# Cross attention, the first head pair's maxima: half the score units copied by ScalarE, and a running maximum by a scan over a PSUM unit and a copied unit

## The chip, the cores and the metric

One core of one Trainium2 chip runs the whole program: six stages of a small perceiver-like network on 128 tokens of width 256 with a context of 12,544 tokens. The metric is the device time of one execution in microseconds (us), as the median of several runs.

## The reference, cut to what matters

The change lies in the fourth stage, the cross attention of the 128 tokens over the 12,544 context tokens, with 16 heads of 16 numbers each. It is an exact softmax attention over the whole context:

```python
def _L1_xattn_ref(q, k, v, Wq, bq, Wo, bo):
    H, E = 16, 16                       # 128 rows of q, 12544 rows of k and v
    qp, kp, vp = ((a @ Wq.T + bq) for a in (q, k, v))      # split into heads
    scores = jnp.einsum('blhe,bshe->bhls', qp, kp)
    attn = jax.nn.softmax(scores / np.sqrt(E), axis=-1)
    out = jnp.einsum('bhls,bshd->blhd', attn, vp)
    return out @ Wo.T + bo

x = x + _L1_xattn_ref(_layernorm(x), ctx_1024, ctx_1024, L1_xattn_Wq, L1_xattn_bq, L1_xattn_Wo, L1_xattn_bo)
```

## The kernel before

The kernel is one program with one instruction list for each engine, and the lists are tied together by counting semaphores: an instruction adds one to a semaphore when it ends, and another engine's list waits until the count is reached. Each engine works through its list in the order in which it is written.

The heads are treated in eight pairs (NG = 8). For each pair s the kernel needs, for each of the 128 query rows and both heads, the largest score over all 12,544 keys, before it can take exponentials. So each pair passes twice over the keys, once for the maxima and once for the exponentials and the weighted sum.

The maxima pass cuts the keys into 28 units (UNITS) of 448 columns (MU). `maximum_group` (L854 on, matmul in L866) lets TensorE multiply a unit: two matmuls, one for each head, that use different rows of the array, into two neighbouring PSUM banks. The ring `max_ring` gives even units banks 0 and 1 and odd units banks 2 and 3 (MAX_SLOTS = (0, 2)). On VectorE `reduce_unit` (L1610 on) waits for the unit (c_max), reduces 2 x 448 scores to two negated maxima in `unit_max` (L1616), and adds one to c_red, for which TensorE waits before it uses the same banks again. After the 28th unit one small reduction (L1622) takes the minimum of the 28 negated maxima to `neg_max` and counts c_hm.

On TensorE `turn_maxima` (L876) waits for c_hm and transposes `neg_max` to one row; ScalarE's `maxima_row` (L1173) copies that row into `q_stack`, so that the second pass's matmuls subtract the maxima by themselves. The second pass is `scores` (L889, TensorE), `exponentials` (L1180, ScalarE) and `weigh` (L905, TensorE).

The order of the whole is written out. TensorE first does the 28 units of pair 0, then the first 4 units of pair 1 (LEAD = 2 groups of two units), then `turn_maxima(0)`. From then on `step_plan` mixes, step by step, three exponential tiles of pair s, their weighing and a few maxima units of pair s + 1. So the maxima of pairs 1 to 7 are taken beside the exponentials of the pair before; those of pair 0 have no such work beside them. ScalarE's first instruction in the stage is `maxima_row(0)`. Before the stage VectorE splits the queries and writes `q_max` (L1602) and `q_stack` (L1604). `prob` is a large SBUF tile of 12 buffers (NPB) that `exponentials` fills; it is unused during pair 0's maxima. SyncE loads the keys (`k_stack`) and values (`vals`) of pairs 0 and 1 ahead; `load_keys` for later pairs waits for scores of the pair whose buffer it takes.

Of the kernel before, what the change touches and what calls it, by code (L numbers as in the profile page):

```python
# [23 lines left out]
ALU = mybir.AluOpType  # L24
ACT = mybir.ActivationFunctionType
AX_X = mybir.AxisListType.X

P = 128
# [8 lines left out]
MIN_START = -3.0e38  # L37
# [19 lines left out]
NG = H // 2  # L57
VW = HD + 1
TILES = S // P
MU = 448  # L60
UNITS = S // MU
# [14 lines left out]
MAX_SLOTS, EXP_BANKS, SUM_BANK = (0, 2), (4, 5, 6), 7  # L76
# [22 lines left out]
def wait_at(eng, sem, value):  # L99

    if isinstance(value, int) and value <= 0:
        return
    eng.wait_ge(sem, value)
# [139 lines left out]
def build_kernel(nc, k_scratch, v_scratch, ones_scratch, ctx_t, x_in, mask_in, const_in, hist_in, l0_in, rows0_in, xw_in, x_bo_in, x_o_in, l1_in, rows1_in, v_in,  # L243
                 tables_in, out):
    with ExitStack() as outer:  # L245
        def sem(name):
            return outer.enter_context(nc.semaphore(name))

        def sb(name, shape, dt=F32, scope=outer):
            return scope.enter_context(nc.sbuf_tensor(name, shape, dt))  # L250


        bank = outer.enter_context(nc.psum_tensor("bank", [P, 8, 512], F32))
# [121 lines left out]
        le = ExitStack()  # L375
# [3 lines left out]
        q_max = sb("q_max", [P, NG, T], F32R, scope=le)  # L379
        q_stack = sb("q_stack", [P, NG, 2 * T], F32R, scope=le)  # L380
        unit_max = sb("unit_max", [P, 2, UNITS, 2], scope=le)
        neg_max = sb("neg_max", [P, 2, 32], F32R, scope=le)
        o_part = sb("o_part", [P, NG, T], scope=le)
        acc = sb("acc", [P, NG, 2, VW], scope=le)
# [3 lines left out]
        prob = sb("prob", [P, NPB, 2, 2 * T], scope=le)  # L388
# [81 lines left out]
        c_max, c_red, c_hm, c_nt = sem("c_max"), sem("c_red"), sem("c_hm"), sem("c_nt")  # L470
        c_sc, c_exp, c_wt = sem("c_sc"), sem("c_exp"), sem("c_wt")
        c_ev, c_ot, c_fill, ld_rows0 = sem("c_ev"), sem("c_ot"), [sem("c_fill0"), sem("c_fill1")], sem("ld_rows0")
        c_ones = sem("c_ones")

        exp_ring = Ring(EXP_BANKS)
        exp_at, turn_at = {}, {}
# [120 lines left out]
        def _(pe):  # L597
# [254 lines left out]
            max_ring = Ring(MAX_SLOTS)  # L852

            def maximum_group(g):  # L854

                s = g // (UNITS // 2)
                for u in (2 * g % UNITS, 2 * g % UNITS + 1):
                    n, at = max_ring.take()
                    wait_at(pe, c_red, max_ring.free(n))
                    if u == 0 and s < 2:  # L860
                        pe.wait_ge(c_fill[s], 32)
                    if u % CHUNK_UNITS == 0:
                        pe.wait_ge(c_stack[s % 2][u // CHUNK_UNITS], 96 * (s // 2 + 1))
                    cols = slice(u * MU, (u + 1) * MU)
                    for hh, rows in ((0, slice(0, 3 * HD + 1)), (1, slice(64, 64 + 3 * HD))):
                        last = nc.tensor.matmul(bank[:, at + hh, 0:MU], q_max[rows, s, :], k_stack[s % 2][rows, cols],  # L866
                                                start=True, stop=True)
                    last.then_inc(c_max, 1)
# [25 lines left out]
            def weigh(e):  # L894

                s, u = divmod(e, EU)
                pe.wait_ge(c_exp, exp_at[e][0] + 1)
                if u == 0:
                    pe.wait_ge(c_vals[s % 2], 16 * (s // 2 + 1))
                    wait_at(pe, c_ev, s)  # L900
                for t in range(2):
                    k = 2 * u + t
                    for hh in range(2):
                        at = 32 * (2 * hh + t)
                        last = nc.tensor.matmul(bank[at:at + 32, SUM_BANK, 0:T],  # L905
                                                vals[:, s % 2, hh, k * VW:k * VW + 32],
                                                prob[:, e % NPB, t, hh * T:(hh + 1) * T],
                                                start=(u == 0), stop=(u == EU - 1))
                last.then_inc(c_wt, 1)

            dve_s.wait(pe, "q_max")
            for g in range(UNITS // 2):
                maximum_group(g)
            for g in range(UNITS // 2, UNITS // 2 + LEAD):
                maximum_group(g)
            turn_maxima(0)
            waiting = []
            for exps, turns, groups in step_plan():
                for e in exps:
                    scores(e)  # L920
                done_now = []
                for e in waiting:
                    if done_now and e % EU == 0:
                        break
                    weigh(e)
                    done_now.append(e)
                waiting = waiting[len(done_now):] + list(exps)
                for s in turns:
                    turn_maxima(s)
                for g in groups:  # L930
                    maximum_group(g)
            for e in waiting:
                weigh(e)
            pe.wait_ge(c_red, NG * UNITS)
            for g in range(NG):
                pe.wait_ge(c_ev, g + 1)
                last = nc.tensor.transpose(bank[:, g // 4, (g % 4) * P:(g % 4 + 1) * P], o_part[:, g, :], ident)
# [74 lines left out]
        def _(act):  # L1012
# [8 lines left out]
            A = nc.scalar.activation  # L1021
# [145 lines left out]
            def maxima_row(s):  # L1167

                n, at = turn_at[s]
                act.wait_ge(c_sc, n + 1)  # L1170
                if s == 0:
                    dve_s.wait(act, "q_stack")
                A(q_stack[MAX_ROW:MAX_ROW + 1, s, :], bank[MAX_ROW:MAX_ROW + 1, at, 0:2 * T],  # L1173
                  ACT.Copy).then_inc(c_exp, 1)
# [8 lines left out]
            def sums_copy(s):  # L1183
                act.wait_ge(c_wt, EU * (s + 1))
                A(o_part[:, s, :], bank[:, SUM_BANK, 0:T], ACT.Copy).then_inc(c_ev, 1)

            maxima_row(0)
            ready = None
            for exps, turns, groups in step_plan():
# [95 lines left out]
        def _(dve):  # L1285
            V = nc.vector
            own = [0]

            def link(ins):

                own[0] += 1
                ins.then_inc(dve_own, 1)
                dve.wait_ge(dve_own, own[0])
# [146 lines left out]
            for b in range(4):  # L1440
# [4 lines left out]
                                            op0=ALU.mult, op1=ALU.mult), f"att0_{b}")  # L1445
# [51 lines left out]
            for b in range(4):  # L1497
# [37 lines left out]
                                        op1=ALU.add), "x2")  # L1535
# [11 lines left out]
                                        op0=ALU.is_equal, op1=ALU.add))  # L1547
# [59 lines left out]

            max_ring = Ring(MAX_SLOTS)

            def reduce_unit(s, u):  # L1610

                n, at = max_ring.take()
                dve.wait_ge(c_max, n + 1)
                if u == 0:
                    wait_at(dve, c_hm, s - 1)
                V.tensor_reduce(unit_max[:, s % 2, u, :], bank[:, at:at + 2, 0:MU], AX_X, ALU.max,  # L1616
                                negate=True).then_inc(c_red, 1)
                if u == UNITS - 1:
                    dve.wait_ge(c_red, n + 1)
                    if s > 0:  # L1620
                        dve.wait_ge(c_sc, turn_at[s - 1][0] + 1)
                    V.tensor_reduce(neg_max[:, :, 0], unit_max[:, s % 2, :, :].rearrange("p u h -> p h u"), AX_X,  # L1622
                                    ALU.min).then_inc(c_hm, 1)

            for s in range(NG):
                for u in range(UNITS):
                    reduce_unit(s, u)

# [21 lines left out]
                                        op0=ALU.mult, op1=ALU.mult), "xr")  # L1650
# [110 lines left out]
```

## Time and profile before

| | |
|---|---|
| median of 3 runs | 1046.29 us (1046.09 to 1048.83) |
| the profiled execution | 1046.74 us, span 1044.7 us |
| mean granted TensorE clock over the span | 0.879 of 2.4 GHz |
| busy: PE, DVE, ACT, POOL | 859.5, 636.5, 541.6, 127.8 us |
| L1616, all 224 reductions of the maxima | 232.4 us |
| L866, the maxima's 448 matmuls | 95.8 us |
| the stretches in time | context pass, whose squares (L1053) run from 18.9 to 396 us; small serial stages until 626; cross attention, whose scores (L889) run from 658.9 to 956; then the serial rest |

PE is TensorE, PEld its weight loads, DVE VectorE, ACT ScalarE, POOL GpSimd, SP SyncE. An engine's busy time is a sum over the span; what bounds a stage has to be read from that stage's own rows. A row of a timeline gives the start, the time from the start of the first to the end of the last instruction in the row, and their count; in brackets stands how long the engine was idle before and what ended that. Ends of matmuls are modelled. [...]

### The profile page before, as it was taken

Reading aid. Unit: us, or ns where it says so; the run is one execution under the profiler, and the core shown is the slowest. Engines: PE = TensorE matmul, PEld = TensorE weight load, DVE = VectorE, ACT = ScalarE, POOL = GpSimd, SP = SyncE. Lnnn points to the kernel's source line nnn. Section 1 sums busy time; section 2 is a strip of 40 time slices with the busy share of each in tenths; the row PEclk is TensorE's granted clock in tenths of the full one; section 3 lists DMA queues with packets and bytes.
Section 4 is the critical chain, followed back from the end, with each engine's and each line's share of the span. In section 5 each row is a group of like instructions: output and inputs, shape, how many; then the busy total and the mean of one; then the engine's idle time right before and its main releaser. Section 6 shows DMA issues by size and latency. Waiting matters only on the chain. (4 is left out here: it accounts for less than half of the span.)

```text
span 1044.7 us, 19625 instructions
## 1 busy us (share of the span) xinstructions
PE 859.5 (82%) x7644; PEld 669.5 (64%) x7644; DVE 636.5 (61%) x1132; ACT 541.6 (52%) x1075; POOL 127.8 (12%) x135
## 2 busy tenths in 40 slices
PE   4999999999999997360065957999999999998756
PEld 4888878788787884240042942677777777776544
DVE  3555566677666676639933449677778778731141
ACT  2776777867768676130021100566666666675010
POOL 2322222222222220008000000000000000000010
PEclk9999999999999998685556885799999999999575
DMA  3465644555545555240029269479979988341000
GB/s 111 129 167 155 173 119 145 135 159 148 144 136 142 134 144 95 104 199 0 0 29 145 42 127 209 85 128 185 190 158 176 179 180 154 96 147 58 1 0 5
DMA packets 83138, 126.26 MB, mean 121 GB/s; under 512 B 10755, under 2 KB 73476, under 8 KB 82246
## 3 DMA queue, kind: packets, MB, share of 16 engines
q1 hardware_dynamic: 83046, 125.01, 50.1%
q8 instruction: 60, 0.98, 0.4%
q14 instruction: 32, 0.26, 0.1%
HBM read 85.46 MB, written 39.52 MB: 120 GB/s over the span
## 5 line engine op out<-in xcount | busy, mean ns | idle before, releaser
L1616 DVE TENSOR_REDUCE unit_max<-bank 128x2 f32<-128x896 f32 x224 | 232.4, 1085 | 64.5 <-PE bank L866 64.3
L1180 ACT ACTIVATE prob<-bank 128x512 f32<-128x512 f32 x392 | 205.8, 598 | 82.4 <-PE bank L889 79.4
L889 PE MATMUL bank<-q_stack,k_stack 112*128 112x256 f32 x784 | 129.2, 300 | 0.7 <-ACT q_stack L1173 0.5
L601 PE MATMUL bank<-hc_high,w_high 128*128 128x256 f32 x392 | 117.6, 300 | 8.6 <-POOL hc_low L1234 8.4
L889 PEld LDWEIGHTS bank<-q_stack,k_stack 112*128 112x128 f32 x784 | 102.3, 190 | 31.5 <-ACT prob L1180 17.6
L1349 DVE SCALAR_TENSOR_TENSOR normed<-bank,b_centered,rstd_wide 128x256 f32<-128x256 f32 x196 | 85.4, 478 | 46.8 <-ACT rstd_wide L1060 46.6
L905 PE MATMUL bank<-prob,vals 128*32 128x128 f32 x3136 | 113.4, 278 | 0.0
L601 PE MATMUL bank<-hc_high,w_low 128*128 128x256 f32 x392 | 112.6, 287 | 0.0
L601 PE MATMUL bank<-hc_low,w_high 128*128 128x256 f32 x392 | 112.3, 286 | 0.0
L866 PE MATMUL bank<-k_stack,q_max 49*128 49x448 f32 x448 | 95.8, 484 | 12.5 <-DVE unit_max L1616 11.1
L1053 ACT ACTIVATE square<-bank,b_centered 128x256 f32<-128x256 f32 x196 | 81.8, 471 | 28.5 <-PE bank L601 28.5
L646 PE MATMUL bank<-eh,hw 128*128 128x512 f32 (+1 forms) x200 | 92.7, 588 | 0.0
L905 PEld LDWEIGHTS bank<-prob,vals 128*32 128x32 f32 x3136 | 78.1, 110 | 17.5 <-ACT prob L1180 0.4
L601 PEld LDWEIGHTS bank<-hc_high,w_high 128*128 128x128 f32 x392 | 76.4, 195 | 9.3 <-issue 9.3
L866 PEld LDWEIGHTS bank<-k_stack,q_max 49*128 49x128 f32 x448 | 43.1, 198 | 54.6 <-DVE unit_max L1616 32.6
L601 PEld LDWEIGHTS bank<-hc_high,w_low 128*128 128x128 f32 x392 | 76.8, 196 | 0.0
L601 PEld LDWEIGHTS bank<-hc_low,w_high 128*128 128x128 f32 x392 | 76.2, 194 | 0.0
L1045 ACT ACTIVATE eh<-normed,hw 128x512 f32<-128x512 f32 (+1 forms) x100 | 74.4, 806 | 0.1
L601 PE MATMUL bank<-hc_high,x_high 128*128 128x256 f32 x196 | 73.1, 373 | 0.0
L1250 POOL TENSOR_TENSOR rstd<-var_eps,half_power 128x1 f32<-128x1 f32 x8 | 4.4, 550 | 552.7 <-DVE var_eps L1408 552.7
L1372 DVE CUSTOM_DVE_ANT_0 eh<-eh,logits 128x1024 f32<-128x1024 f32 (+1 forms) x52 | 59.4, 1161 | 17.2 <-POOL h_rstd L1239 13.8
L1234 POOL TENSOR_TENSOR hc_low<-hc_raw,hc_high 128x512 fp32r<-128x512 f32 x49 | 62.4, 1273 | 46.4 <-DVE group_stats L1372 45.2
(299 smaller groups left out, 1287.4 us busy)
## 6 DMA issues: line engine op xcount, KB each, us to landing
k_stack<-k_scratch SPq DMA_DIRECT2D x336, 112.0 KB, 5.1
vals<-v_scratch SPq DMA_DIRECT2D x8, 1666.0 KB, 10.3
v_scratch<-vst SPq DMA_DIRECT2D x12, 1088.0 KB, 9.5
hc_raw<-in_ctx_t SPq DMA_DIRECT2D x49, 256.0 KB, 3.1
k_scratch<-k_high SPq DMA_DIRECT2D x49, 256.0 KB, 3.4
k_scratch<-k_low SPq DMA_DIRECT2D x49, 256.0 KB, 3.5
w_ffn<-in_l SPq DMA_DIRECT2D x4, 1920.0 KB, 13.8
w_l<-in_l SPq DMA_DIRECT2D x6, 603.0 KB, 5.4
```

The source lines that it names most:

```text
L601: last = nc.tensor.matmul(out_ap, lhs, rhs, start=(n == 0), stop=(n == len(pairs) - 1))
L646: last = nc.tensor.matmul(bank[:, 5, 0:width], w1_hist[:, c, :], eh[:, gb, c, at:at + width], start=(c == 0), stop=(c == CT - 1))
L866: last = nc.tensor.matmul(bank[:, at + hh, 0:MU], q_max[rows, s, :], k_stack[s % 2][rows, cols], start=True, stop=True)
L889: last = nc.tensor.matmul(bank[:, at, t * 2 * T:(t + 1) * 2 * T], k_stack[s % 2][0:STACK, k * P:(k + 1) * P], q_stack[0:STACK, s, :], star ...
L905: last = nc.tensor.matmul(bank[at:at + 32, SUM_BANK, 0:T], vals[:, s % 2, hh, k * VW:k * VW + 32], prob[:, e % NPB, t, hh * T:(hh + 1) * T ...
L1045: A(eh[:, group % 2, c, at:at + width], normed[:, i % 2, c, 0:width], ACT.Gelu, bias=v_hist["beta"][:, c:c + 1], scale=v_hist["g"][:, c:c ...
L1053: ins = A(square[:, c, :], bank[:, 2 * (n % 2) + half, (c % 2) * CH:(c % 2 + 1) * CH], ACT.Square, bias=b_centered[:, c:c + 1])
L1180: A(prob[:, e % NPB, :, :], bank[:, at, :].rearrange("p (u t) -> p u t", u=2), ACT.Exp).then_inc(c_exp, 1)
L1234: TT(hc_low[:, b], hc_raw[:, b], hc_high[:, b].bitcast(F32), ALU.subtract).then_inc(h_low, 1)
L1349: V.scalar_tensor_tensor(out=normed[:, n // 2 % 2, c, at:at + CH], in0=bank[:, 2 * b + half, (c % 2) * CH:(c % 2 + 1) * CH], scalar=b_cent ...
L1372: V.tensor_tensor_reduce(part_of, part_of, logits[:, gb, lo:lo + width], 1.0, 0.0, ALU.mult, ALU.add, group_stats[:, group, half * CT + c: ...
L1616: V.tensor_reduce(unit_max[:, s % 2, u, :], bank[:, at:at + 2, 0:MU], AX_X, ALU.max, negate=True).then_inc(c_red, 1)
```

## The change

Pair 0's maxima are taken in another way; those of pairs 1 to 7 stay as they are. The 28 units of pair 0 go in 14 iterations of an even and an odd unit. ScalarE copies the odd unit (2 x 448 scores of each row) from banks 2 and 3 to one of two places in `prob` (`unit_copy`). VectorE then runs two scans, one for each head. A scan goes over 448 positions and keeps a running maximum: state = max(max(state, even unit in PSUM), odd unit's copy in SBUF); it writes the running values to `prob` (`running`), and the next iteration's scan starts from the last of them. After the 14th iteration two small copies gather the two last values in `first_best`, and a multiplication by -1 writes `neg_max` and counts c_hm.

TensorE's waits change with it: an even unit waits for the scans that read the banks before (c_scan), an odd unit for the copy that read its banks (c_copy). The count c_red now starts with pair 1.

```diff
+        def unit_copy(i):
+            lo = 2 * (i % 2)
+            flat = prob[:, lo:lo + 2, :, :].rearrange("p b u t -> p (b u t)")
+            return flat[:, 0:2 * MU].rearrange("p (h k) -> p h k", h=2)
+
+        def running(i, hh):
+            return prob[:, 4 + 2 * (i % 2) + hh, :, :].rearrange("p u t -> p (u t)")[:, 0:MU]
...
                     n, at = max_ring.take()
-                    wait_at(pe, c_red, max_ring.free(n))
+                    if s == 0 or n - len(MAX_SLOTS) < UNITS:
+                        freed = n // 2
+                        if u % 2 == 0:
+                            wait_at(pe, c_scan, 2 * freed)
+                        else:
+                            wait_at(pe, c_copy, freed)
+                    else:
+                        wait_at(pe, c_red, max_ring.free(n) - UNITS)
...
+            for i in range(UNITS // 2):
+                act.wait_ge(c_max, 2 * i + 2)
+                wait_at(act, c_scan, 2 * (i - 1))
+                A(unit_copy(i), bank[:, MAX_SLOTS[1]:MAX_SLOTS[1] + 2, 0:MU], ACT.Copy).then_inc(c_copy, 1)
             maxima_row(0)
...
+            for i in range(UNITS // 2):
+                max_ring.take()
+                max_ring.take()
+                dve.wait_ge(c_copy, i + 1)
+                for hh in range(2):
+                    if i > 0:
+                        dve.wait_ge(c_scan, 2 * i + hh - 1)
+                    V.tensor_tensor_scan(out=running(i, hh), data0=bank[:, MAX_SLOTS[0] + hh, 0:MU],
+                                         data1=unit_copy(i)[:, hh, :],
+                                         initial=MIN_START if i == 0 else running(i - 1, hh)[:, MU - 1:MU],
+                                         op0=ALU.max, op1=ALU.max).then_inc(c_scan, 1)
+            for hh in range(2):
+                dve.wait_ge(c_scan, UNITS - 1 + hh)
+                link(V.tensor_copy(first_best[:, hh:hh + 1], running(UNITS // 2 - 1, hh)[:, MU - 1:MU]))
+            V.tensor_scalar(neg_max[:, :, 0], first_best[:, :], -1.0, None, ALU.mult).then_inc(c_hm, 1)
...
-            for s in range(NG):
+            for s in range(1, NG):
                 for u in range(UNITS):
                     reduce_unit(s, u)
```

## Rows read from the trace of the kernel before

**Rows 1.** Busy time of the engines by stretch, with the granted clock and the DMA share.
```profile
core 0: us, PE busy (x) PEld busy (x) DVE busy (x) ACT busy (x) POOL busy (x), PEclk, DMA share, GB/s
...
626.40:654.60 28.20, 20.12 (x56) 7.87 (x56) 28.16 (x30) 0.00 (x0) 0.00 (x0) 0.52 0.98 205
654.60:658.50 3.90, 3.10 (x10) 1.28 (x10) 3.90 (x5) 0.01 (x1) 0.00 (x0) 0.50 0.01 5
...
658.00:662.00 4.00, 3.27 (x14) 2.53 (x13) 0.67 (x1) 3.48 (x6) 0.00 (x0) 0.50 0.00 0
...
666.00:670.00 4.00, 4.00 (x64) 2.85 (x62) 3.41 (x4) 2.66 (x6) 0.00 (x0) 1.00 0.95 167
...
720.00:760.00 40.00, 39.63 (x578) 28.63 (x573) 31.50 (x32) 27.15 (x54) 0.00 (x0) 1.00 0.90 175
```

**Rows 2.** Waits, 622 to 660 us: who for whom, us in total, times, longest.
```profile
ACT q_stack L1173 <- PE bank L876: 54.5, 1, 54.5
...
PE bank L866 <- DVE unit_max L1616: 10.8, 30, 3.1
```

**Rows 3.** Timeline of the first maxima: start us, us, engine, line, op, tiles, count, idle before.
```profile
623.77 2.60 DVE L1604 TENSOR_SCALAR q_stack<-bank,const 128x1024 fp32r<-128x1024 f32 x2
...
623.79 0.68 PE L866 MATMUL bank<-k_stack,q_max 49*128 49x448 f32 x4 [1.39 <-DVE q_max L1602]
626.40 28.03 DVE L1616 TENSOR_REDUCE unit_max<-bank 128x2 f32<-128x896 f32 x28
...
627.55 0.74 PE L866 MATMUL bank<-k_stack,q_max 49*128 49x448 f32 x2 [3.09 <-DVE unit_max L1616]
...
628.55 0.74 PE L866 MATMUL bank<-k_stack,q_max 49*128 49x448 f32 x2 [0.26 <-DVE unit_max L1616]
...
654.47 0.21 DVE L1622 TENSOR_REDUCE neg_max<-unit_max 128x2 fp32r<-128x56 f32 x1
...
656.73 0.74 PE L866 MATMUL bank<-k_stack,q_max 49*128 49x448 f32 x2 [0.26 <-DVE unit_max L1616]
...
657.40 1.06 PE L876 MATMUL bank<-const,neg_max 128*32 128x128 f32 x4
658.50 0.37 ACT L1173 ACTIVATE q_stack<-bank 1x256 fp32r<-1x256 f32 x1 [54.50 <-PE bank L876]
```

**Rows 4.** The matmuls of the maxima from 640 to 680 us: ns smallest, median, largest.
```profile
L866 PE MATMUL bank<-k_stack,q_max x60: 378/737/741, 639.5 to 676.5; 49*128 49x448 f32 x30, 48*128 48x448 f32 x30
```

**Rows 5.** VectorE by line and shape: count, busy us, mean ns, idle us before.
```profile
L1616 DVE TENSOR_REDUCE unit_max<-bank 128x2 f32<-128x896 f32 x224 | 232.4, 1085 | 64.5 <-PE bank L866 64.3
...
L1349 DVE SCALAR_TENSOR_TENSOR normed<-bank,b_centered,rstd_wide 128x256 f32<-128x256 f32 x196 | 85.4, 478 | 46.8 <-ACT rstd_wide L1060 46.6
...
L1560 DVE TENSOR_TENSOR hid<-silu,bank 128x512 f32<-128x512 f32 x5 | 3.4, 687 | 13.3 <-ACT silu L1163 13.3
...
L1434 DVE TENSOR_TENSOR k_blocks<-bank,const 128x1024 f32<-128x1024 f32 x2 | 2.4, 1224 | 0.1
...
L1524 DVE RECIPROCAL den<-bank 128x256 f32<-128x256 f32 x1 | 1.8, 1758 | 2.2 <-PE bank L788 2.2
...
L1516 DVE TENSOR_TENSOR h_beta<-bank,w_l 128x256 f32<-128x256 f32 x1 | 0.4, 425 | 9.4 <-ACT q_sig L1153 9.4
```

**Rows 6.** ScalarE by line and shape, columns as in group 5.
```profile
L1130 ACT ACTIVATE att<-bank 128x512 f32<-128x512 f32 x8 | 4.8, 597 | 10.1 <-PE bank L728 10.1
...
L1124 ACT ACTIVATE kT<-bank 128x256 f32<-128x256 f32 x1 | 0.4, 383 | 18.7 <-PE bank L601 18.7
```

**Rows 7.** Instructions in order of time, where engines hand over, 559 to 588 us.
```profile
582.72 4.74 PE L601 MATMUL bank<-xT,w_ffn 128*128 128x128 f32 x40
...
583.92 0.60 ACT L1163 ACTIVATE silu<-bank 128x512 f32<-128x512 f32 x1 [3.40 <-PE bank L601]
584.62 0.69 DVE L1560 TENSOR_TENSOR hid<-silu,bank 128x512 f32<-128x512 f32 x1 [4.03 <-ACT silu L1163]
...
587.50 0.60 ACT L1163 ACTIVATE silu<-bank 128x512 f32<-128x512 f32 x1 [2.98 <-PE bank L601]
```

More of the change, by code:

```diff
@@ L381, in build_kernel @@
         unit_max = sb("unit_max", [P, 2, UNITS, 2], scope=le)
+        first_best = sb("first_best", [P, 2], scope=le)
         neg_max = sb("neg_max", [P, 2, 32], F32R, scope=le)
@@ L473, in build_kernel @@
         c_ones = sem("c_ones")
+        def unit_copy(i):
[4 more added lines that the diff above has]
+            return prob[:, 4 + 2 * (i % 2) + hh, :, :].rearrange("p u t -> p (u t)")[:, 0:MU]
+        c_copy, c_scan = sem("c_copy"), sem("c_scan")
         exp_ring = Ring(EXP_BANKS)
@@ L933, in _ @@
                 weigh(e)
-            pe.wait_ge(c_red, NG * UNITS)
+            pe.wait_ge(c_red, (NG - 1) * UNITS)
             for g in range(NG):
@@ L1618, in reduce_unit @@
                 if u == UNITS - 1:
-                    dve.wait_ge(c_red, n + 1)
+                    dve.wait_ge(c_red, n + 1 - UNITS)
                     if s > 0:
```

## The prediction

> **What bounds the kernel now.** I read the busy times by stretch first, then the waits of the stretch that the change touches, then its timeline. In the 28.20 us in which the first pair's maxima are taken, VectorE is busy for 28.16 us and ScalarE for none, while TensorE has 20.12 us of work at a granted clock of 0.52, its lower level, 1.2 GHz [rows 1]. ScalarE's first instruction of the attention waits 54.5 us for the transposed maxima, and TensorE's idle time in the stage, 10.8 us in 30 waits, is ended by VectorE's reductions [rows 2]. The timeline shows the rhythm: 28 reductions in 28.03 us, back to back, and a pair of matmuls after each, 0.74 us long, at 627.55 and again 1.00 us later [rows 3]. Two units are in flight, one in banks 0 and 1, one in 2 and 3; while VectorE reads one, TensorE fills the other. So VectorE alone sets the stage's length, nothing runs beside it that could hide anything, and what is saved or lost in it moves the end one for one. The loop behind it has TensorE busy for 39.63 of 40 us at full clock [rows 1]; the change does not touch its instructions. (The page's chain of waits names only a few per cent of the span, so I do not use it.)
>
> **The change part by part.** It removes 28 reductions and their last reduction over units, and adds 14 ScalarE copies of 128x896, 28 scans over 448 elements, and three small VectorE instructions. More important is the order that it makes. Number the iterations i, with an even unit E(i) and an odd unit O(i).
> - TensorE's E(i) waits for both scans of iteration i-1 (the even unit stays in PSUM until they have read it). O(i) waits only for copy i-1, but stands behind E(i) in TensorE's queue.
> - Copy i waits for O(i).
> - Both scans of iteration i wait for copy i.
>
> Each waits for the one before, in a ring: scans, E, O, copy, scans. Nothing of iteration i+1 can run beside anything of iteration i. The period is thus a sum where it was a maximum. Its terms:
>
> *Scans.* No row shows a scan. Each combines 448 elements of PSUM with 448 of SBUF and carries a running value, two maxima per element, the second of which feeds the next element's first. Lower bound: a plain two-operand instruction of this length. 256 elements take 0.425 us, 512 take 0.687, 1024 take 1.224 [rows 5], so 1.04 ns each and about 0.16 fixed; 448 make 0.62 us, the two of an iteration 1.25. Upper bound: two such instructions for each scan, 2.50 for an iteration. I take two steps per element, one after the other because of the feedback: 896 steps, as many as the reduction of 896 elements has, which takes 1.08 us [rows 5]. Two scans: 2.16 us. (They may overlap by 0.08 us, as reductions do, 28 x 1.08 = 30.2 against 28.03 [rows 3, 5]; their start value comes through a pointer, and the instruction with a pointer scalar takes 0.478 us where the plain one takes 0.425 [rows 5], 0.05 each. The two cancel.) The value lies nearest to the reduction's row, the only one with a value carried from element to element; the reduction has one step of feedback and the scan has two.
>
> The Trainium skill, "DVE: opcode table, instruction layouts, handler registers and perf-mode slots", section 6, says that the built-in scan routes its result back to an earlier stage and runs at half throughput; no row of this case shows a scan, so this can't be compared. By it the pair costs about what I took and VectorE is not relieved at all; the lower bound would then be out of reach.
>
> *From VectorE to TensorE.* A reduction starts at 626.40 and ends 1.08 later, at 627.48; the matmuls start at 627.55 [rows 3, 5]: 0.07 us.
>
> *E and O.* A matmul here takes 0.737 us at the lower clock and 0.378 at the higher [rows 4]; the two of a unit run side by side on different rows, 0.74 us for both [rows 3]. In the ring TensorE has less work per microsecond than now, and its clock is at the lower level even now, so I let it stand there: 2 x 0.74 = 1.48 us. At the higher level it would be 0.74 (four matmuls in 0.68 us at 623.79 [rows 3]).
>
> *From TensorE to ScalarE.* Matmuls end at 587.46, the activation starts at 587.50 [rows 7]: 0.04 us.
>
> *Copy.* 256 elements from PSUM take 0.383 us, 512 take 0.597 [rows 6]: 0.84 ns each more; 896 make 0.597 + 384 x 0.84 ns = 0.92 us.
>
> *From ScalarE to VectorE.* An activation ends at 584.52, VectorE's product starts at 584.62 [rows 7]: 0.10 us.
>
> Gap between two iterations' scans: 0.07 + 1.48 + 0.04 + 0.92 + 0.10 = 2.61 us. Period 4.77 us where two reductions take 2.00 now. The first copy costs nothing: units 0 and 1 are multiplied at 623.79 and VectorE still writes q_stack until 626.37 [rows 3], so scan 0 starts at 626.40 as the first reduction does; without that cover it would cost 1.0 us once. Stage: 14 x 2.16 + 13 x 2.61 = 30.2 + 33.9 = 64.2 us against 28.03: **+36.1 us**.
>
> *The tail.* Two copies of one element and a multiplication follow the scans, each at most the 0.21 us of the small reduction that they replace [rows 3], and they are hidden: TensorE first has to multiply unit 28. Now unit 28 and 29 are refilled while the last reductions run; after the change they start at the end of the last scan. From there: 0.07 + 0.74, hand-over 0.10, reduction 28 to 1.99, reduction 29 to 2.98, unit 31's matmuls from 3.05 to 3.79, where the transposes follow in TensorE's queue. Now the last reduction ends at 626.40 + 28.03 = 654.43 and the transposes start at 657.40, as unit 31's matmuls end [rows 3]: 2.97 us. **+0.8 us**. Queued behind the new waits are, on TensorE, the second pair's first four units and these transposes; on VectorE, the second pair's reductions; on ScalarE, only the maxima row, which comes last anyhow.
>
> *Elsewhere.* SyncE's loads for later pairs wait for scores and move with them. The transfers of the stage (DMA share 0.98) are finished before 654.60, where the share is 0.01 [rows 1]; a longer stage gives them room that nobody needs. The clock comes back after the stage as now: 0.50 from 658 to 662 us, 1.00 from 666 [rows 1]. Less work on TensorE before could delay that by a microsecond; I put it at nothing.
>
> Sum: +36.9 us. The profiled execution took 1046.74 us (span 1044.7), 0.45 above the median of the runs, 1046.29. 1046.74 + 36.9 = 1083.6 against the profiled one, **1083.2** against the median. With scans at their upper bound, 14 x 0.34 = 4.8 more: 1088. These ends belong to the same case.
>
> **The rivals.**
> 1. *The scan runs at one step per element.* For it: every two-operand row does, also one with two operations per element (0.478 us for 256 [rows 5]). Against it: those carry nothing from element to element. The ring stays: 14 x 1.25 + 33.9 = 51.4 us, +23.4, with the tail +24.2: 1070.5. It contradicts the skill's half throughput.
> 2. *The higher clock in the ring.* TensorE's work would shrink by 0.74 us in 13 gaps: 9.6 less, and 0.7 in the tail, with slow scans 1073. Against it: the 0.52 of the stage now.
> 3. *The scan is much dearer.* One kind of VectorE instruction takes over 6 ns per element, the reciprocal: 1758 ns for 256 [rows 5]. A scan like it would take 0.16 + 448 x 6.25 ns = 2.96 us, the pair 5.9, 14 x 3.8 = 53 us more than forecast: 1136. Nothing but that one row speaks for it. Three steps per element would be 1.56 us, 1083 + 14 x 0.96 = 1097.
> 4. *The other side: the odd unit's path hides behind the scans.* If O(i+1) and copy i+1 ran beside the scans of i, the ring would shrink to scans, hand-over, E, hand-over. At one step per element and the higher clock that is 1.25 + 0.07 + 0.37 + 0.10 = 1.79 us, the stage 25.1, with the tail's 0.8 a gain of 2: 1044. It decides in TensorE's queue, and below a period of (28.03 - 0.8) / 14 = 1.95 us. At two steps it is not reached in any order: 2.16 alone is more. Against it: TensorE runs in the order written, and E(i+1) stands ahead.
>
> Even scans of no length would leave 13 x 2.61 = 33.9 us, more than the 28.03 of now; so slower is nearly sure.
>
> **How the numbers follow.** Forecast (ring with two steps per element or up to two instructions' worth) 0.76; rival 1 0.13; rival 2 0.03; rival 3, over 1090, 0.06; rival 4 0.02. The likeliest gives 1083. The range of 1069 to 1090 holds the forecast and rivals 1 and 2. A measurement tells about 0.3% (3 us) from no change: slower 0.98, the same 0.01, faster 0.01, the last two from rival 4.
>
> **What would show it.** In the profile of the changed kernel the stage from 626.4 us should be 64 us long, with 14 groups of two scans 4.8 us apart; the scan near 1.08 us (0.62 for rival 1); L866's pairs two by two, 0.74 us each, right behind the scans; the new copy 0.92 us, starting 0.04 after them; VectorE busy for about 30 of 64 us, its idle time ended by ScalarE; the granted clock near 0.5. The loop behind should be as long as before. The prediction is wrong if copies are seen beside scans, if the matmuls run at half the duration, or if the stage's loss does not appear at the end.

## The result, and the profile after

The changed kernel takes 1079.99 us (median; 1079.61 to 1081.59) where the kernel before took 1047.56 beside it: a ratio of 1.031, 95% interval 1.028 to 1.034. In a later comparison the same pair gave 1.030 (1.028 to 1.033). The prediction was 1083 us, slower; the loss was 32.4 us where 36.9 were forecast.

The profiled execution took 1081.59 us, its span 1079.5. The timeline shows the ring as it was described (columns as in [rows 3]; first the start of the stretch, then one iteration, then the end and the tail):

```profile
627.76 2.60 DVE L1626 TENSOR_SCALAR q_stack<-bank,const 128x1024 fp32r<-128x1024 f32 x2
...
627.78 0.68 PE L884 MATMUL bank<-k_stack,q_max 49*128 49x448 f32 x4 [1.39 <-DVE q_max L1624]
...
628.49 0.92 ACT L1208 ACTIVATE prob<-bank 128x896 f32<-128x896 f32 x1 [20.49 <-PE bank L884]
...
630.39 2.07 DVE L1639 TENSOR_TENSOR_SCAN prob<-bank,prob 128x448 f32<-128x448 f32 x2
...
632.52 1.12 PE L884 MATMUL bank<-k_stack,q_max 49*128 49x448 f32 x4 [4.07 <-DVE prob L1639]
633.67 0.92 ACT L1208 ACTIVATE prob<-bank 128x896 f32<-128x896 f32 x1 [4.26 <-PE bank L884]
...
680.40 1.11 PE L884 MATMUL bank<-k_stack,q_max 49*128 49x448 f32 x4 [3.24 <-DVE prob L1639]
681.56 0.92 ACT L1208 ACTIVATE prob<-bank 128x896 f32<-128x896 f32 x1 [3.44 <-PE bank L884]
682.51 2.19 DVE L1639 TENSOR_TENSOR_SCAN prob<-bank,prob 128x448 f32<-128x448 f32 x2 [2.16 <-ACT prob L1208]
...
684.76 1.12 PE L884 MATMUL bank<-k_stack,q_max 49*128 49x448 f32 x4 [3.24 <-DVE prob L1639]
...
686.87 2.19 DVE L1639 TENSOR_TENSOR_SCAN prob<-bank,prob 128x448 f32<-128x448 f32 x2 [2.16 <-ACT prob L1208]
...
689.11 1.11 PE L884 MATMUL bank<-k_stack,q_max 49*128 49x448 f32 x4 [3.23 <-DVE prob L1639]
689.35 0.17 DVE L1646 TENSOR_SCALAR neg_max<-first_best 128x2 fp32r<-128x2 f32 x1
689.90 4.08 DVE L1654 TENSOR_REDUCE unit_max<-bank 128x2 f32<-128x896 f32 x4 [0.38 <-PE bank L884]
...
692.71 1.06 PE L894 MATMUL bank<-const,neg_max 128*32 128x128 f32 x4
693.80 0.38 ACT L1191 ACTIVATE q_stack<-bank 1x256 fp32r<-1x256 f32 x1 [6.97 <-PE bank L894]
```

From 680.40 on each row starts where the one before ends: four matmuls, the copy, two scans, and the next four matmuls at 684.76, 4.36 us after the last ones. Inside the ring no two of the three engines work at a time. The scans begin at 630.39 and `neg_max` is computed at 689.35, 58.96 us; in the kernel before the same stretch took 28.07 (626.40 to 654.47 [rows 3]).

By line and shape, and by wait, from 622 to 695 us (columns as in [rows 5] and [rows 2]):

```profile
L1639 DVE TENSOR_TENSOR_SCAN prob<-bank,prob 128x448 f32<-128x448 f32 x28 | 30.6, 1133 | 28.1 <-ACT prob L1208 28.1
L884 PE MATMUL bank<-k_stack,q_max 49*128 49x448 f32 x32 | 17.7, 645 | 48.6 <-DVE prob L1639 46.2 <-DVE q_max L1624 1.4 <-DVE unit_max L1654 1.1
...
L1208 ACT ACTIVATE prob<-bank 128x896 f32<-128x896 f32 x14 | 12.8, 917 | 66.0 <-PE bank L884 66.0
...
PE bank L884 <- DVE prob L1639: 46.2, 14, 4.1
DVE prob L1639 <- ACT prob L1208: 28.1, 13, 2.2
```

VectorE has 30.6 us of scans, more than the 28.03 us of reductions that they replace [rows 3], and now waits 28.1 us for ScalarE; TensorE waits 46.2 us for the scans. The clock, by stretch (columns as in [rows 1]):

```profile
630.30:689.10 58.80, 14.48 (x52) 6.51 (x52) 30.66 (x30) 11.92 (x13) 0.00 (x0) 0.51 0.47 98
...
698.00:702.00 4.00, 4.00 (x38) 2.79 (x38) 1.93 (x2) 1.39 (x4) 0.00 (x0) 0.50 0.00 0
702.00:706.00 4.00, 4.00 (x62) 2.91 (x62) 2.28 (x4) 2.31 (x5) 0.00 (x0) 0.89 1.08 174
```

The stretch runs almost wholly at the lower clock, 0.51 on the mean, as it did before (0.52 [rows 1]).

How the 34.8 us between the two profiled spans divide, from the starts in the timelines:

| stretch | before | after | |
|---|---|---|---|
| up to the first reduction or scan | 626.40 | 630.39 | +4.0 |
| from there to `neg_max` | 28.07 | 58.96 | +30.9 |
| `neg_max` to the row of maxima (ScalarE, `q_stack`) | 4.03 | 4.45 | +0.4 |
| row of maxima to the first copy of sums, the loop's first pair | 43.83 | 45.00 | +1.2 |
| the loop's other seven sums | 255.0 | 255.3 | +0.3 |
| last copy of sums to the end | 87.35 | 85.40 | -1.9 |

The first line needs no cause in the change; experiment 5 shows why.

### The profile page after: what moved, and what is told of

Same layout as the page of the kernel before. It is cut to its first block and busy times, and to the rows that moved or that the text cites. A ratio compares the mean times of both kernels' runs of the same rounds, so it can differ in the third digit from the quotient of the medians.

```text
span 1079.5 us, 19667 instructions
## 1 busy us (share of the span) xinstructions
PE 857.6 (79%) x7644; PEld 671.8 (62%) x7644; DVE 639.5 (59%) x1134; ACT 554.4 (51%) x1089; POOL 127.8 (12%) x135
## 5 line engine op out<-in xcount | busy, mean ns | idle before, releaser
L1654 DVE TENSOR_REDUCE unit_max<-bank 128x2 f32<-128x896 f32 x196 | 204.5, 1086 | 66.2 <-PE bank L884 66.0
L884 PE MATMUL bank<-k_stack,q_max 49*128 49x448 f32 x448 | 90.4, 473 | 49.0 <-DVE prob L1639 46.2
```

## The experiments

The "stretch" is always the time from the first reduction or scan to `neg_max`; "before" is the median of runs on the same chip.

### 1. Is it the ring? The odd unit first, alone and with the copy doubled

```diff
-                for u in (2 * g % UNITS, 2 * g % UNITS + 1):
...
+                for u in (units[::-1] if s == 0 else units):
...
-                act.wait_ge(c_max, 2 * i + 2)
+                act.wait_ge(c_max, 2 * i + 1)
...
                 dve.wait_ge(c_copy, i + 1)
+                dve.wait_ge(c_max, 2 * i + 2)
```

> Only the order of TensorE's list is changed for pair 0: the odd unit O(i+1) stands ahead of the even unit E(i+1), ScalarE's copy waits for the odd unit alone and VectorE's scans for the copy and the even unit. Theory (the ring of scans, E, O, copy sets the period): O and the copy now run beside the scans of the iteration before, so the period falls from 4.36 us (changed kernel) to scans 2.19 + hand-over 0.07 + E 0.74 + hand-over 0.10 = 3.10 us, the stretch of the scans from 58.7 to about 42.5 us, and the time to 1063 to 1064 us (before + 15 to 16). Rival (the scans' own length is what was lost, the order does not matter): VectorE's scans take 30.7 us in either order, so 1080 us as the changed kernel.

Measured: ratio 1.018 (1.016 to 1.020), 1068.9 us against 1050.4 before; stretch 42.49 us. The timeline:

```profile
645.01 2.19 DVE L1643 TENSOR_TENSOR_SCAN prob<-bank,prob 128x448 f32<-128x448 f32 x2 [0.89 <-PE bank L887]
645.33 0.92 ACT L1211 ACTIVATE prob<-bank 128x896 f32<-128x896 f32 x1 [2.17 <-PE bank L887]
...
647.26 1.11 PE L887 MATMUL bank<-k_stack,q_max 49*128 49x448 f32 x4 [1.97 <-DVE prob L1643]
648.10 2.19 DVE L1643 TENSOR_TENSOR_SCAN prob<-bank,prob 128x448 f32<-128x448 f32 x2 [0.90 <-PE bank L887]
648.41 0.92 ACT L1211 ACTIVATE prob<-bank 128x896 f32<-128x896 f32 x1 [2.17 <-PE bank L887]
```

The copy starts 0.32 us after the scans and runs beside them; the period is 3.09 us. The 16.5 us that the stretch lost against the changed kernel come from moving one unit in a queue, with the same 28 scans. The rival (only the scans' length counts) falls. The time fell by 1.3% or 13 us, less than the stretch: in the profiles the loop's first pair is 4.0 us longer than in the changed kernel and the serial end 2.0 us longer (table in experiment 5).

In the second kernel each copy is made twice:

```diff
+                link(A(unit_copy(i), bank[:, MAX_SLOTS[1]:MAX_SLOTS[1] + 2, 0:MU], ACT.Copy))
                 A(unit_copy(i), bank[:, MAX_SLOTS[1]:MAX_SLOTS[1] + 2, 0:MU], ACT.Copy).then_inc(c_copy, 1)
```

> As e1_odd_first, and ScalarE makes every copy of pair 0 twice, one after the other (0.92 + about 0.95 us). Theory: in e1 the copy has the whole of the scans and of E as cover (3.1 us, against 0.37 + 0.04 + 1.9 + 0.10 = 2.4 us needed), so the time is that of e1 within 1 us. Rival (the copy adds its time wherever it stands, by contention for PSUM or SBUF or by its semaphores): e1 + 12 us.

Measured: ratio 1.018 (1.015 to 1.020), stretch 42.50 us. The 13 us of added copies (14 of 0.92 us) cost nothing. The same edit to the changed kernel:

> The changed kernel with every copy of pair 0 made twice. Theory (ring): the second copy is a term of the period; 13 x 0.95 = 12.4 us more than the changed kernel, about 1092 us, period 5.3 us. Rival (copies are hidden beside VectorE, whose scans are the loss): 1080 us.

Measured: ratio 1.039 (1.037 to 1.042), stretch 71.27 us, 12.3 more than the changed kernel's, where 12.4 were expected:

```profile
645.84 0.92 ACT L1208 ACTIVATE prob<-bank 128x896 f32<-128x896 f32 x1 [3.44 <-PE bank L884]
646.79 0.92 ACT L1209 ACTIVATE prob<-bank 128x896 f32<-128x896 f32 x1
647.74 2.19 DVE L1640 TENSOR_TENSOR_SCAN prob<-bank,prob 128x448 f32<-128x448 f32 x2 [3.11 <-ACT prob L1209]
...
649.98 1.12 PE L884 MATMUL bank<-k_stack,q_max 49*128 49x448 f32 x4 [4.18 <-DVE prob L1640]
651.14 0.92 ACT L1208 ACTIVATE prob<-bank 128x896 f32<-128x896 f32 x1 [3.44 <-PE bank L884]
```

The same work is free in one order and costs in full in the other; that is what "on the path" means.

### 2. The ring opened by a second place for even units

```diff
+                        if s == 0 and u % 4 == 2:
+                            at = EXP_BANKS[0]
                         if u % 2 == 0:
-                            wait_at(pe, c_scan, 2 * freed)
+                            wait_at(pe, c_scan, 2 * freed - 2)
...
-                    V.tensor_tensor_scan(out=running(i, hh), data0=bank[:, MAX_SLOTS[0] + hh, 0:MU],
+                    V.tensor_tensor_scan(out=running(i, hh), data0=bank[:, (MAX_SLOTS[0], EXP_BANKS[0])[i % 2] + hh, 0:MU],
```

> The changed kernel with even units alternating between banks 0, 1 and 4, 5, so that E(i) waits for the scans of iteration i-2 and no longer for those of i-1; nothing else is changed. Theory: the ring is opened; the period is the longer of the scans, 2.19 us, and 0.07 + 1.12 + 0.04 + 0.92 + 0.10 = 2.25 us; the stretch of the scans about 31.4 us, the time before + 4 us, 1051 to 1052 us. It cannot fall below before + 2.6, since 28 scans take 30.7 us where the 28 reductions took 28.0. Rival (another wait or contention holds the copies and scans apart): a stretch of 42 us or more.

Measured: ratio 1.004 (1.002 to 1.005), stretch 30.57 us. The scans now follow each other almost without a gap:

```profile
639.13 11.92 DVE L1641 TENSOR_TENSOR_SCAN prob<-bank,prob 128x448 f32<-128x448 f32 x11
...
640.32 1.12 PE L886 MATMUL bank<-k_stack,q_max 49*128 49x448 f32 x4 [1.16 <-DVE prob L1641]
641.47 0.92 ACT L1210 ACTIVATE prob<-bank 128x896 f32<-128x896 f32 x1 [1.36 <-PE bank L886]
...
L1641 DVE TENSOR_TENSOR_SCAN prob<-bank,prob x28: 1065/1125/1150, 629.5 to 658.6; 128x448 f32<-128x448 f32 x28
```

Eleven scans in 11.92 us are 1.08 us each. VectorE is busy with scans for 29.8 us and waits 0.5 us between them, so this is close to its own bound, and it still lies above the 28.07 us of the reductions. So the loss of 30.9 us has two parts: 28.4 us belong to the ring. The other 2.5 us are 1.8 us of longer work (29.8 us of scans against 28.0 of reductions), the 0.5 us of short waits and the small instructions behind the last scan. A scan over 448 positions, which takes in two operands, costs a little more than the reduction of 896 elements: the copy has relieved VectorE of nothing.

### 3. What a scan costs: a plain maximum in its place

```diff
-                    V.tensor_tensor_scan(out=running(i, hh), data0=bank[:, MAX_SLOTS[0] + hh, 0:MU],
-                                         data1=unit_copy(i)[:, hh, :],
-                                         initial=MIN_START if i == 0 else running(i - 1, hh)[:, MU - 1:MU],
-                                         op0=ALU.max, op1=ALU.max).then_inc(c_scan, 1)
+                    V.tensor_tensor(running(i, hh), bank[:, MAX_SLOTS[0] + hh, 0:MU],
+                                    unit_copy(i)[:, hh, :], ALU.max).then_inc(c_scan, 1)
```

> The changed kernel with each scan replaced by a plain elementwise maximum of the same two operands, written to the same place, without a running value; so the maxima are only those of the last iteration's columns, position 447. Theory: a scan makes two steps per element and the plain maximum one, 0.62 us each (448 x 1.04 ns + 0.16), a pair of them 1.17 to 1.25; the ring stays with its gap of 2.17 us: stretch 14 x 1.2 + 13 x 2.17 = 45 us, 13.5 less than the changed kernel's 58.7, so about 1066 us. Even then the ring is 17 us longer than the 28 reductions. Rival (the operands cost the time, PSUM beside a fresh SBUF copy, not the scan): as the changed kernel, 1080 us.

Measured: ratio 1.017 (1.014 to 1.020), stretch 44.57 us. The two rows, nanoseconds smallest, median and largest:

```profile
L1639 DVE TENSOR_TENSOR_SCAN prob<-bank,prob x28: 1065/1127/1150, 630.4 to 687.9; 128x448 f32<-128x448 f32 x28
...
L1639 DVE TENSOR_TENSOR prob<-bank,prob x28: 614/620/625, 629.4 to 673.0; 128x448 f32<-128x448 f32 x28
```

Same two operands, same output, 0.620 us against 1.07 to 1.09 for the two scans that start from a constant and 1.12 to 1.15 for those that start from a value in SBUF (median of all 1.127). With 0.16 us of fixed time in both, an estimate from the row of 256 and 1024 elements [rows 5], the plain operation goes through one element per 1.03 ns and the scan through one per 2.1 to 2.2, so the operands are not what costs. This agrees with the half throughput that the Trainium skill states (DVE: opcode table, instruction layouts, handler registers and perf-mode slots, section 6). Even with this cheap instruction the ring is 16.5 us longer than the reductions.

### 4. The same aim without scan and ring

If ScalarE's copies are to relieve VectorE, what VectorE does with a copy has to be cheaper than reducing the unit. Two kernels copy as bfloat16 (the maxima only shift the exponents, and the same rounded value is used throughout a row) and fold copies elementwise into a running maximum; the other units are reduced from PSUM. Four pairs of banks are used, so that a refill can run beside other work. VectorE's part of the second, in which two units of three are copied and DIRECT = 10 reduced (cut to its main loop):

```diff
+            def fold(p):
+                dve.wait_ge(c_copy, 2 * p + 2)
+                wait_at(dve, c_scan, p - 1)
+                V.tensor_tensor(copies(0), copies(0), copies(p), ALU.max).then_inc(c_scan, 1)
...
+            for k in range(DIRECT):
+                dve.wait_ge(c_max, 3 * k + 1)
+                V.tensor_reduce(unit_max[:, 0, k, :], bank[:, 0:2, 0:MU], AX_X, ALU.max, negate=True).then_inc(c_red, 1)
+                if k > 1:
+                    fold(k - 1)
...
```

> Pair 0 without a scan and without a ring: even units are reduced from PSUM as in the kernel before (banks 0, 1 and 4, 5 in turn), odd units (banks 2, 3 and 6, 7) are copied by ScalarE as bfloat16, and VectorE folds each copy into a running elementwise maximum in SBUF, which one reduction ends. Theory: VectorE alone sets the length; 14 reductions at 1.00 us and 13 folds of 896 elements. If a fold makes one step per element, as all float32 rows do (1.09 us), the stretch is 29.6 us and the time that of before + 1.5 us. The Trainium skill, VectorE: DVE Perf Modes, the tier table, gives an elementwise operation on 2-byte operands in SBUF two elements per step; by it a fold takes 0.63 us, the stretch 23.8 us, and the time is 4 us (0.4%) less than before. I expect the second.

Measured: stretch 22.37 us, 5.7 less than before, and yet a ratio of 1.000 (0.998 to 1.002); in a second comparison, experiment 5, 0.999 (0.998 to 1.001). Here the expectation missed: 4 us less were expected, and the time did not follow the stretch.

> As the mixed kernel before it, but of every three units ScalarE copies two and VectorE reduces one; two copies are folded by one instruction of 1792 elements, 10 reductions and 8 folds in all, then a fold of the two halves and one reduction. With two elements per step a fold takes 1.09 us: 10 x 1.00 + 8 x 1.13 + 0.65 + 1.1 + 0.2 = 21 us for the stretch, 7 us less than before, a time of 0.993 of before. With one element per step: 28.5 us, the same as before. ScalarE then has 18 copies at 0.92 us, 16.6 us of work, and is covered.

Measured: ratio **0.993** (0.991 to 0.996), stretch 21.76 us, 6.3 less than before. It beats both kernels, as expected. The first four rows are of this kernel, then comes the fold of the kernel before it (L1639), last that of this one (L1646):

```profile
632.81 1.08 DVE L1650 TENSOR_REDUCE unit_max<-bank 128x2 f32<-128x896 f32 x1
633.11 1.73 ACT L1217 ACTIVATE prob<-bank 128x896 bf16<-128x896 f32 x2 [0.21 <-PE bank L891]
633.81 1.08 DVE L1646 TENSOR_TENSOR prob<-prob 128x1792 bf16<-128x1792 bf16 x1
...
633.95 1.49 PE L891 MATMUL bank<-k_stack,q_max 49*128 49x448 f32 x6 [0.51 <-DVE unit_max L1650]
...
L1639 DVE TENSOR_TENSOR prob<-prob x13: 614/615/625, 629.5 to 647.0; 128x896 bf16<-128x896 bf16 x13
...
L1646 DVE TENSOR_TENSOR prob<-prob x8: 1080/1083/1084, 631.8 to 645.8; 128x1792 bf16<-128x1792 bf16 x8
```

A reduction at 632.81 and a fold at 633.81 (two copies at once) alternate without a gap, while ScalarE copies and TensorE multiplies beside them. (In the first iterations, where there is no fold yet, VectorE waits twice, 0.84 us each, for TensorE.) A fold of 896 bfloat16 elements takes 0.615 us and one of 1792 takes 1.083, 0.52 ns per element: two per step, as the tier table of the Trainium skill (VectorE: DVE Perf Modes) has it for 2-byte operands.

### 5. What the clock adds: second profiles

> The changed kernel once more, unaltered, for a second profile. Theory: the stretch of the scans (58.7 us) and the tail behind it (4.5 us) come out the same within 0.1 us, while the stretch ahead of it (626 to 631 us in the kernels so far) and the 85 to 87 us behind the last loop move by some us with the moment at which the granted clock rises. Rival: the stretch ahead is longer in the changed kernel by its own doing, then it starts at 630 us again.

> The kernel before, unaltered, for a second profile. In the first one the reductions began at 626.4 us, in two profiles of the changed kernel the scans began at 630.4 and 631.5. Theory (the stretch ahead varies with the moment at which the clock rises, in every kernel): the reductions may begin anywhere from 626 to 632 us; the 28 reductions take 28.1 us again and the loop's first pair after the row of maxima 43.8 us. Rival (the change itself lengthens the stretch ahead): 626.4 again.

> The mixed kernel (every second unit copied as bfloat16 and folded), unaltered, for a second profile. Its stretch was 22.4 us, 5.7 less than before, and its time that of before. Theory: the gain is given back by the clock, which rises late in the loop's first pair (50.6 us from the row of maxima to the first sum, where the kernel before takes 43.8), and does so again: 49 us or more. Rival: the late rise was chance, then about 44 us and a time 5 us below before.

> The kernel with two of three units copied, unaltered, for a second profile and a second ratio. Theory: stretch 21.8 us, first pair 43.8 us as in its first profile, ratio 0.993 again. Rival (the ratio came from a lucky clock): first pair 49 us and a ratio near 1.

Measured, in us, first and second profile of each kernel:

| kernel | stretch begins at | stretch | loop's first pair | last sums to end |
|---|---|---|---|---|
| before | 626.40, 629.35 | 28.07, 28.06 | 43.83, 43.83 | 87.4, 87.3 |
| changed | 630.39, 631.54 | 58.96, 58.95 | 45.00, 45.01 | 85.4, 85.4 |
| odd unit first (second: copy doubled) | 626.61, 631.79 | 42.49, 42.50 | 49.01, 49.01 | 87.4, 87.4 |
| every second unit folded | 626.45, 631.08 | 22.37, 22.37 | 50.56, 49.02 | 83.0, 84.6 |
| two of three folded | 626.95, 626.04 | 21.76, 21.76 | 43.77, 43.76 | 87.0, 87.1 |

Ratios of the second comparisons: changed 1.030, before 1.000 (0.999 to 1.002), every second folded 0.999 (0.998 to 1.001), two of three folded 0.994 (0.992 to 0.996). So the late clock behind "every second unit folded" came again, and so did the gain of "two of three".

Where the stretch begins varies within one kernel. The kernel before, first and second profile, ten microseconds of the small serial stages:

```profile
550.00:560.00 10.00, 6.72 (x26) 3.40 (x24) 1.57 (x5) 2.40 (x4) 0.00 (x0) 0.84 0.88 133
...
550.00:560.00 10.00, 7.93 (x17) 3.95 (x16) 0.69 (x2) 1.95 (x4) 0.00 (x0) 0.50 0.95 146
```

With a granted clock of 0.84 there the reductions begin at 626.40, with 0.50 at 629.35. All 13 profiles divide in this way: 0.84 goes with a start at 626 to 627, 0.50 with one at 629 to 632, and two unaltered kernels, the one before and the one with every second unit folded, had both. So the start moves by 3 us and more without any change, and the +4.0 us of the first line of the table above can be chance. Both profiles of the changed kernel had the late start (630.39, 631.54); that it starts late more often than the others is not excluded by two profiles.

The loop's first pair is another matter: it repeats within 0.01 us for most kernels, and differs between them. The time from 4 us behind the start of the row of maxima on, in steps of 4, first the kernel "every second unit folded" (row at 652.82), then "two of three" (row at 652.70):

```profile
656.80:660.80 4.00, 4.00 (x35) 2.85 (x34) 1.72 (x2) 1.40 (x4) 0.00 (x0) 0.50 0.00 0
660.80:664.80 4.00, 4.00 (x35) 2.85 (x34) 2.03 (x3) 1.51 (x4) 0.00 (x0) 0.50 0.95 174
664.80:668.80 4.00, 4.00 (x36) 2.83 (x34) 2.03 (x3) 1.51 (x5) 0.00 (x0) 0.50 0.02 2
...
656.70:660.70 4.00, 4.00 (x61) 2.88 (x60) 1.83 (x2) 1.95 (x5) 0.00 (x0) 0.77 0.09 27
660.70:664.70 4.00, 4.00 (x52) 2.90 (x52) 3.41 (x5) 2.37 (x5) 0.00 (x0) 1.00 0.90 148
```

TensorE is busy without a gap in all of them, but in the first kernel the clock is still at its lower level, 0.50, 16 us after the row of maxima; in the second it is at 1.00 after 8. The same reading in all 13 profiles, the mean granted clock of the 24 us from the start of the row of maxima:

| mean granted clock of these 24 us | loop's first pair, us | profiles |
|---|---|---|
| 0.87 to 0.88 | 43.8 to 43.9 | before (both), plain maximum, two of three folded (both) |
| 0.81 | 45.0 | changed (both) |
| 0.78 | 45.6, 45.7 | copy doubled in the changed kernel, second place for even units |
| 0.61 | 49.0 | odd unit first (both), every second unit folded (second) |
| 0.54 | 50.6 | every second unit folded (first) |

The later the clock rises, the longer the pair, without an exception, and the instructions of the loop are the same in all of them. For the kernel with every second unit folded that is 5.2 to 6.7 us more than before, against the 5.7 that the stretch had saved; the odd unit first pays 5.2 us against the kernel before and 4.0 against the changed one.

Two things stay open. One is why the clock rises late behind some stretches and not behind others: no run here changed that moment alone. The other is the whole account of the kernel with every second unit folded. Its serial end is 2.8 to 4.3 us shorter than before, at a mean granted clock of 0.67 to 0.68 in place of 0.64, so that from the start of the stretch to the end both its profiles are 3 us shorter than those of the kernel before. The two ratios say 0.4 and 0.7 us less, give or take 2. Where its stretch begins, 626 or 631 us, may weigh in its medians, but the profiles are too few to tell.

## Why the prediction was right, and what it mis-sized

- **What bounds the stage**: right. Nothing hid the change; 30.9 us more in the stretch moved the end by 32.4 in the median.
- **The ring**: right, and shown by experiments 1 and 2. Moving O ahead of E gave 42.49 us where the sum of terms expected 42.5, and a second place for even units 30.57 where 31.4 were expected. These sums, made before the runs, used the hand-overs and matmul times that the changed kernel's profile had shown.
- **Scans**: forecast 1.08 each, 2.16 for two; measured 2.07 for the first two and 2.19 for those that take their start value from SBUF. The two small effects that I let cancel did not quite: 0.4 us over 14 iterations. Two steps per element was right; rival 1 (one step) and rival 3 (three steps and more) are both excluded by the scans' own row, and experiment 3 shows what one step costs on the same operands, 0.62 us.
- **E and O**: this is the mis-sized term. I took 2 x 0.74 = 1.48 us; four matmuls take 1.12, and six take 1.49 (633.95 in experiment 4). So each unit right behind another adds only 0.37 us, which is 448 columns at 1.2 GHz, and the other 0.37 us of the first unit is paid once for the whole row; what fills it no run here shows. Ends of matmuls are modelled, but the copy confirms the sum: it starts 1.16 us after the first of the four (680.40, 681.56). The error is 0.36 x 13 = 4.7 us, most of the 5.5 us by which the stretch was over-estimated (64.2 against 58.7, from 630.39 to the last scan's end at 689.06). The four matmuls in 0.68 us at 623.79 [rows 3], less than twice the 0.378 of [rows 4], hinted at it.
- **Copy and hand-overs**: copy 0.92, as forecast. ScalarE to VectorE took 0.03 us (the copy at 681.56 ends at 682.48, the scans start at 682.51), not 0.10: 0.9 us in all. The gap is 0.06 + 1.11 + 0.05 + 0.92 + 0.03 = 2.17 us (the rows at 680.40 to 682.51), not 2.61. The first copy was hidden under `q_stack`, as forecast (628.49 to 629.41, VectorE free at 630.36).
- **The tail**: +0.8 forecast. The last scan ends at 689.06 and the transposes start at 692.71, 3.65 us against 2.97 before: +0.7. The small instructions were hidden behind unit 28.
- **Elsewhere at nothing**: not quite. The loop's first pair took 1.2 us more, the clock reaching its upper level later (0.50 from 698 to 702, 4 to 8 us after the row of maxima), and the serial end 1.9 us less, both repeated in the second profile. They nearly cancel, which is luck. The cause of the shorter end is not shown. That I named this term ("a microsecond") and set it to zero was right only by its size here; in experiment 1 and in the first kernel of experiment 4 the same term is 5 to 7 us.
- **Rival 2** (higher clock in the ring): excluded by the 0.51. **Rival 4** (copies beside scans): in TensorE's written order it can't be; experiment 1 wrote the other order, and it still lost. There the even unit is still refilled between the scans, 0.90 us in a period of 3.09, and the 2.19 us of scans alone are more than the 2.00 of two reductions.
- **The time itself** came out nearer than the sum deserved: 3.2 us from the 1083.2, while the stretch was 5.2 us shorter than forecast. The kernel before measured 1.3 us more beside the changed one (1047.56) than the 1046.29 from which the forecast started, and the median loss, 32.4 us, is 1.6 above what the profiles add up to without the first line of the table (30.8), well inside its interval.

## What to carry to other kernels

Before work is handed to another engine, write down who waits for whom through one iteration, and include the place in each queue: if every wait closes on the one before, the period is the sum of the engines' times, and one more buffer or one exchanged pair of instructions can be worth more than a faster instruction (here 28.4 and 16.5 us of the stretch, against 14.4 for a plain maximum in place of the scan). Then ask what the relieved engine still has to do with the handed-over part; a scan that took in a unit's half and its partner's copy cost as much as the reduction of a whole unit, an elementwise maximum on 2-byte copies a little over half as much (0.615 against 1.085 us for 896 elements). And a gain in front of a dense stretch has to be read at the end of it, since the clock can take it back.

## What the runs showed of the hardware

- `tensor_tensor_scan` over 448 float32, one operand in PSUM: 1.07 to 1.09 us with a constant start value, 1.12 to 1.15 with a start value from SBUF; 1.08 each in a row of eleven. A plain maximum of the same operands: 0.620.
- Units of two matmuls of 448 columns at the lower clock: one alone takes 0.74 us, two in a row 1.12, three 1.49.
- The elementwise maximum of 896 bfloat16 elements in SBUF takes 0.615 us, of 1792 elements 1.083.
- After pair 0's stretch the granted clock was at its upper level 8 us after the row of maxima in some kernels and not yet after 16 us in others, although TensorE was busy without a gap from 4 us on. It was much the same in two profiles of one kernel, and worth up to 6.7 us.
